# One stacked matmul of depth 96 instead of three for the destination term of a graph-network message

## The reference

```
m_in  = concat([x[src], x[dst], edge_attr])        # 200000 x 384
m     = silu(m_in @ msg_W1 + b1) @ msg_W2 + b2
agg   = segment_sum(m, dst)                        # sorted dst
x_new = LN(x + LN(x + mlp([x, agg])))
```

## Time and profile before

| | |
|---|---|
| median of three runs | 2572.13 us |
| span of the profiled execution | 2569.7 us |
| TensorE matmuls busy | 2182.9 us (85%), 21030 |
| weight loads busy | 1871.4 us (73%) |
| VectorE busy | 1577.3 us (61%) |
| ScalarE busy | 847.9 us (33%) |
| GpSimd busy | 1664.2 us (65%) |
| mean granted TensorE clock | 0.919 |
| DMA | 471.71 MB, mean 184 GB/s |

### The profile page before, as it was taken

How to read it: one execution, slowest core, us unless ns; L and a number is a source line. 1 busy time by engine, 2 the same in 40 slices (tenths; PEclk the granted TensorE clock), 3 DMA queues, 4 the chain that set the end, 5 groups by cost and what they waited for, 6 DMA issues and landing times. The chain is left out here.

```text
span 2569.7 us, 58924 instructions
## 1 busy us (share of the span) xinstructions
PE 2182.9 (85%) x21030; PEld 1871.4 (73%) x21030; DVE 1577.3 (61%) x4059; ACT 847.9 (33%) x1368; POOL 1664.2 (65%) x1618
## 2 busy tenths in 40 slices
PE   7898888888888988898889888988898878799996
PEld 7786777677777776776777776767677754699994
DVE  4786676667666766676667666766676647600005
ACT  3343333333333433333333333333333326200004
POOL 4777777777777777777777777777777755200002
PEclk9899999899899989998899999999999988899998
DMA  6555545554555555545554555455545543688871
GB/s 236 197 190 190 167 159 185 181 169 154 177 190 173 158 180 181 187 141 180 184 190 139 186 175 190 144 182 176 191 150 176 176 118 96 245 309 302 303 268 51
DMA packets 135225, 471.71 MB, mean 184 GB/s; under 512 B 55730, under 2 KB 77490, under 8 KB 113555
## 3 DMA queue, kind: packets, MB, share of 16 engines
q1 hardware_dynamic: 84586, 368.35, 41.1%
q0 software_dynamic: 50176, 102.86, 14.3%
q10 hardware_dynamic: 426, 0.03, 0.0%
HBM read 369.41 MB, written 101.70 MB: 183 GB/s over the span
## 5 line engine op out<-in xcount | busy, mean ns | idle before, releaser
L519 POOL DMA_INDIRECT gath<-P_d,src_i x1540 | 1543.2, 1002 | 469.4 <-issue 465.5
L650 PE MATMUL ps_pre<-wc,eT 128*128 128x128 f32 x3136 | 702.4, 306 | 13.7 <-DVE counts L567 13.7
L682 PE MATMUL ps_sum<-h,edgeN 128*128 128x129 f32 x3136 | 486.2, 302 | 265.7 <-ACT h L744 265.2
L590 DVE TENSOR_TENSOR pre<-ps_pre,gath 128x512 f32<-128x512 f32 x392 | 265.9, 678 | 588.6 <-issue 548.7
L682 PEld LDWEIGHTS ps_sum<-h,edgeN 128*128 128x128 f32 x3136 | 422.2, 209 | 278.1 <-ACT h L744 277.7
L744 ACT ACTIVATE h<-pre 128x512 f32<-128x512 f32 x392 | 247.9, 632 | 1122.2 <-DVE pre L590 1068.3
L666 PE MATMUL ps_cnt<-edgeK,edgeL 128*128 128x500 bf16 (+1 forms) x3136 | 585.1, 336 | 29.6 <-DVE edgeK L580 29.4
L580 DVE TENSOR_SCALAR edgeK<-iota,key 128x600 bf16<-128x600 f16 (+2 forms) x1568 | 526.4, 396 | 0.0
L652 PE MATMUL ps_pre<-Qw,nodeE 128*128 128x128 bf16 x4704 | 520.4, 220 | 0.0
L650 PEld LDWEIGHTS ps_pre<-wc,eT 128*128 128x128 f32 x3136 | 478.1, 192 | 32.6 <-issue 29.6
L666 PEld LDWEIGHTS ps_cnt<-edgeK,edgeL 128*128 128x128 bf16 x3136 | 320.1, 105 | 199.3 <-DVE edgeK L580 42.8
(11 more groups left out here) (128 smaller groups left out, 1021.4 us busy)
## 6 DMA issues: line engine op xcount, KB each, us to landing
eT<-eT SPq DMA_DIRECT2D x56, 1792.0 KB, 9.2
A_d<-counts SPq DMA_DIRECT2D x56, 1568.0 KB
A_c<-A_d SPq DMA_DIRECT2D x56, 1568.0 KB, 8.1
rel_b<-rel_d SPq DMA_DIRECT2D x56, 896.0 KB
gath<-P_d,src_i POOLq DMA_INDIRECT x1568
Qw<-Q_d SPq DMA_DIRECT2D x56, 96.0 KB
Q_d<-Qst SPq DMA_DIRECT2D x7, 672.0 KB, 7.8
xT_sb<-xT SPq DMA_DIRECT2D x7, 448.0 KB, 8.1
```

The lines of the kernel that those rows point to most:

```text
L519: pool.indirect_dma_start(gath[:, q, t * D:(t + 1) * D], None, v["P_d"], bass.IndirectOffsetOnAxis(ap=src_i[k][:, c:c + 1], axis=0)).then_ ...
L590: V.tensor_tensor(pre[x][:], ps_pre[x][:], gath[:, q, :], ALU.add).then_inc(pre_add, 1)
L650: T.matmul(o, eT[k][:, e0:e0 + P], wc[:], start=True, stop=False)
L682: last = T.matmul(ps_sum[k][:, 0:SW], edgeN[x][:, t, :], h[x][:, t, 0:SW], start=(q == 0 and t == 0), stop=(q == GQ - 1 and t == QT - 1))
```

## The change

Q_d keeps its layout. Instead of 128 table rows for a group, the kernel now loads 32 rows for each quad, at the quad's own first destination (qbase, a new row of 392 numbers), and puts the three bf16 parts below each other: part t on partitions 32t to 32t+31, so Qw is 96 x 7 x 128. rel_d counts from the quad's first destination, and nodeE has 96 partitions: partition p is compared with p mod 32 (pid is made by an integer iota and an AND), so each edge has three ones in its column. One matmul over 96 partitions then adds all three parts. The window is loaded by 7 register loads and 21 DMAs of 32 x 128 bf16.

The making of rel_d is cut for this into 98 rows of four quads. The core of the diff:

```
-        pid = sb("pid", [P, 1])
+        pid_i, pid = sb("pid_i", [P, 1], I32), sb("pid", [P, 1])
...
-            rel_b = sb("rel_b", [P, GE], BF16, both)
+            rel_b = sb("rel_b", [KQ, GE], BF16, both)
...
-    RP = 2 * GROUPS
-    RC = EP // RP
+    RP, RQ = 98, 4
+    RC = RQ * QT * P
...
-            V.tensor_scalar(relR[:], R_i[:, 0:RC], RB_i[:, 0:1], None, ALU.subtract).then_inc(rel_ready, 1)
+            V.tensor_tensor(rows4(relR[:]), rows4(R_i[:, 0:RC]),
+                            RB_i[:].unsqueeze(2).broadcast_to([RP, RQ, QT * P]), ALU.subtract).then_inc(rel_ready, 1)
...
+            V.tensor_scalar(qbase[:].rearrange("p (g q) -> p g q", q=GQ), F1, 0.0, float(NP_ - 1), ALU.max, ALU.min)
...
+        link(V.tensor_scalar(pid_i[:], pid_i[:], QW - 1, None, ALU.bitwise_and))
+        V.tensor_copy(pid[:], pid_i[:])
...
-    nodeE = [sb(f"nodeE{k}", [P, GE], BF16) for k in range(2)]
-    Qw = [sb(f"Qw{k}", [P, 3 * D], BF16) for k in range(2)]
+    nodeE = [sb(f"nodeE{k}", [KQ, GE], BF16) for k in range(2)]
+    Qw = [sb(f"Qw{k}", [KQ, GQ, D], BF16) for k in range(2)]
...
-            base = sp.value_load(gbase[0:1, bass.ds(g, 1)], min_val=0, max_val=NP_ - 1)
-            sp.dma_start(Qw[k][:], v["Q_d"][bass.ds(base, P), :]).then_inc(q_in[k], 16)
+            for q in range(GQ):
+                base = sp.value_load(qbase[0:1, bass.ds(g * GQ + q, 1)], min_val=0, max_val=NP_ - 1)
+                rows = v["Q_d"][bass.ds(base, QW), :].rearrange("r (t n) -> t r n", t=3)
+                for t in range(3):
+                    sp.dma_start(Qw[k][t * QW:(t + 1) * QW, q, :], rows[t]).then_inc(q_in[k], 16)
...
-                pe.wait_ge(q_in[k], 16 * (half + 1))
+                pe.wait_ge(q_in[k], 3 * GQ * 16 * (half + 1))
...
-                for part in range(3):
-                    last = T.matmul(o, nodeE[k][:, e0:e0 + P], Qw[k][:, part * D:(part + 1) * D],
-                                    start=False, stop=(part == 2))
+                last = T.matmul(o, nodeE[k][:, e0:e0 + P], Qw[k][:, q, :], start=False, stop=True)
```

More of the change, by code:

```diff
@@ L43 @@
 GW = 120
+QW = 32
+KQ = 3 * QW
 LASTQ = P - W0
@@ L82, in bass_gnn_two_layers @@
         gbase = sb("gbase", [1, GROUPS], I32)
+        qbase = sb("qbase", [1, QUADS], I32)
         ident = sb("ident", [P, P])
         identb = sb("identb", [P, P], BF16)
-        pid = sb("pid", [P, 1])
+        pid_i, pid = sb("pid_i", [P, 1], I32), sb("pid", [P, 1])
         iota = sb("iota", [P, 1000], F16)
@@ L146, in build_prepare @@
     P_d, Q_d, rel_d = v["P_d"], v["Q_d"], v["rel_d"]
-    pid, ident, identb, iota = v["pid"], v["ident"], v["identb"], v["iota"]
-    flag, offs, gbase = v["flag"], v["offs"], v["gbase"]
+    pid_i, pid, ident, identb, iota = v["pid_i"], v["pid"], v["ident"], v["identb"], v["iota"]
+    flag, offs, gbase, qbase = v["flag"], v["offs"], v["gbase"], v["qbase"]
     wab = sb("wab", [P, 2, D])
@@ L152, in build_prepare @@
     b1bc = sb("b1bc", [P, D])
-    RP = 2 * GROUPS
-    RC = EP // RP
-    R_i, RB_i, relR = sb("R_i", [RP, RC + 1], I32), sb("RB_i", [RP, 1], I32), sb("relR", [RP, RC], BF16)
+    RP, RQ = 98, 4
+    RC = RQ * QT * P
+    R_i, RB_i, relR = sb("R_i", [RP, RC + 1], I32), sb("RB_i", [RP, RQ], I32), sb("relR", [RP, RC], BF16)
     falls = sb("falls", [RP, RC], BF16)
@@ L189, in sync @@
         rows = v["dst_row"]
-        for h in range(2):
-            half = bass.AP(rows.tensor, rows.offset + h * RC, [[2 * RC, GROUPS], [1, RC + 1]])
-            sp.dma_start(R_i[h * GROUPS:(h + 1) * GROUPS, :], half).then_inc(r_in, 16)
+        sp.dma_start(R_i[:], bass.AP(rows.tensor, rows.offset, [[RC, RP], [1, RC + 1]])).then_inc(r_in, 16)
         for to, a in ((mw2, v["mW2"]), (v["u1a"], v["uW1"][0:D, :]), (u1b, v["uW1"][D:2 * D, :]), (v["u2"], v["uW2"])):
@@ L206, in sync @@
         sp.wait_ge(rel_ready, 1)
-        sp.dma_start(rel_d.rearrange("(g h c) -> h g c", h=2, c=RC)[0], relR[0:GROUPS, :]).then_inc(st_r, 16)
-        sp.dma_start(rel_d.rearrange("(g h c) -> h g c", h=2, c=RC)[1], relR[GROUPS:RP, :]).then_inc(st_r, 16)
+        sp.dma_start(rel_d.rearrange("(r c) -> r c", c=RC), relR[:]).then_inc(st_r, 16)
         for c in range(CHUNKS):
@@ L213, in sync @@
             if c == 1:
-                sp.wait_ge(st_r, 32)
-                sp.dma_start(v["rel_b"][:], rel_d[0:GE].partition_broadcast(P)).then_inc(v["r_in"], 16)
+                sp.wait_ge(st_r, 16)
+                sp.dma_start(v["rel_b"][:], rel_d[0:GE].partition_broadcast(KQ)).then_inc(v["r_in"], 16)
             if c == 3:
@@ L221, in gpsimd @@
     def gpsimd(pool):
-        pool.iota(pid[:], [[0, 1]], base=0, channel_multiplier=1, allow_small_or_imprecise_dtypes=True).then_inc(made, 1)
+        pool.iota(pid_i[:], [[0, 1]], base=0, channel_multiplier=1).then_inc(made, 1)
         pool.iota(iota[:], [[1, 1000]], base=0, channel_multiplier=0, allow_small_or_imprecise_dtypes=True).then_inc(made, 1)
@@ L279, in scalar @@
         firsts, lasts = v["dst_first"], v["dst_last"]
[L280 to L283, removed]
+        with nc.allow_non_contiguous_dma(reason="one word for each quad"):
+            act.dma_start(RB_i[:], firsts[0:TILES].rearrange("(r q t) -> r q t", q=RQ, t=QT)[:, :, 0]).then_inc(r_in, 16)
         act.dma_start(F_i[:], bass.AP(firsts.tensor, firsts.offset, [[GT, GROUPS], [1, GT + 1]])).then_inc(t_in, 16)
@@ L334, in checks @@
             V.memset(bad[:], 0.0)
[L335 to L336 removed]
+            dve.wait_ge(r_in, 32)
+            rows4 = lambda t: t.rearrange("p (q e) -> p q e", q=RQ)
+            V.tensor_tensor(rows4(relR[:]), rows4(R_i[:, 0:RC]),
+                            RB_i[:].unsqueeze(2).broadcast_to([RP, RQ, QT * P]), ALU.subtract).then_inc(rel_ready, 1)
             link(V.tensor_tensor(falls[:], R_i[:, 0:RC], R_i[:, 1:RC + 1], ALU.is_gt))
@@ L368, in checks @@
             V.tensor_scalar(gbase[:], F1[:, :, 0], 0.0, float(NP_ - 1), ALU.max, ALU.min)
+            V.tensor_scalar(qbase[:].rearrange("p (g q) -> p g q", q=GQ), F1, 0.0, float(NP_ - 1), ALU.max, ALU.min)
+        dve.wait_ge(made, 1)
+        link(V.tensor_scalar(pid_i[:], pid_i[:], QW - 1, None, ALU.bitwise_and))
+        V.tensor_copy(pid[:], pid_i[:])
         dve.wait_ge(b_in, 16)
@@ L400, in settled @@
         eng.wait_ge(st_z, 16)
-        eng.wait_ge(st_r, 32)
+        eng.wait_ge(st_r, 16)
         for stored, ring in ((st_p, PR), (st_q, QR)):
@@ L409, in build_edges @@
 def build_edges(nc, ctx, sem, sb, v):
-    flag, offs, gbase, force_general = v["flag"], v["offs"], v["gbase"], v["force_general"]
+    flag, offs, gbase, qbase, force_general = v["flag"], v["offs"], v["gbase"], v["qbase"], v["force_general"]
     pid, ident, identb, iota, wc = v["pid"], v["ident"], v["identb"], v["iota"], v["wc"]
@@ L478, in load_rel @@
         def load_rel(g):
-            sp.dma_start(rel_b[:], v["rel_d"][bass.ds(g * GE, GE)].partition_broadcast(P)).then_inc(r_in, 16)
+            sp.dma_start(rel_b[:], v["rel_d"][bass.ds(g * GE, GE)].partition_broadcast(KQ)).then_inc(r_in, 16)
         def store(g, k):
@@ L552, in expand @@
         def expand(k, cols):
-            return V.tensor_scalar(nodeE[k][:, cols], rel_b[:, cols], pid[:, 0:1], None, ALU.is_equal)
+            return V.tensor_scalar(nodeE[k][:, cols], rel_b[:, cols], pid[0:KQ, 0:1], None, ALU.is_equal)
         def expand_first(half, k, early=False):
```

## The result

| | before | changed |
|---|---|---|
| median us (lowest to highest, runs) | 2572.76 (2570.74 to 2574.09, 4) | 2751.97 (2748.25 to 2755.56, 4) |
| ratio, 95% interval | | 1.0694, 1.0678 to 1.071 |
| profiled run: time, span us | 2572, 2569.7 | 2750.08, 2748.2 |
| mean granted TensorE clock | 0.919 | 0.859 |
| last edge sums end, us | 2102.35 | 2282.47 |

The kernel is 6.9% slower; 2767 was forecast. The whole loss lies ahead of the last edge sums.

The account below looks back on a forecast made before the run. GpSimd's gathers bound the kernel at 36.6 us a group; the change makes a 39.8 us loop through SyncE's store, paid 54 times. With the later start, 195 us added to 2572.1 gives 2767 us, range 2690 to 2850.

Parts of the forecast that it names:

- SyncE's list: SyncE's issues after each group: 7 register loads and 21 DMAs add 14.5 us, so the store goes out at S+17.7.
- Rivals 3 and 4: Window loads: 0.71 us issue each, 2972 us (9%); or each waiting for the one before to land, near 4650 (2%).
- rival 4: Window loads: each small load waits for the one before to land, loop 75 us, time near 4650 us; chance 2%.
- The store's landing: Store of counts in each group: lands 13.0 us after its issue, and the next memset of counts waits for it.
- The loop: Each edge group: list, store, memset, rest of group (9.0 us) close a loop of 39.8 us, 3.2 above GpSimd's 36.6.
- One sign: Edge loop: GpSimd would now wait for adds, as one mark of the closed loop; no size given.
- The start: Prelude: longer lists start TensorE 13.9 us later, at 90.4; GpSimd loses 10.7 us; first S comes at 121.9.
- The sum: End of the last edge sums: 2296.9 us, 194.6 later than before, giving 2767 us in all.
- The matmuls: TensorE in the edge part: removed matmuls save 0.45 us a quad, 3.2 us a group, lying in spare time.
- rival 2: Edge part: TensorE's chain sets the pace, so the removed matmuls pay 176 us and the time is 2407; chance 5%.
- gathers' 36.6: GpSimd in the edge loop: a group's 28 gathers cost 36.6 us, the shortest group once its head start is used.
- rival 1: Edge loop: GpSimd stays the bound and only the start is paid, 2583 us, 0.4% slower; chance 14%.

Follow-up runs that it names:

- e1: Changed kernel with the store of counts issued right behind src_i, ahead of the window's 21 loads and eT: 2654.82 us, ratio 1.0326.
- e3: Kernel before the change, with 22 further register loads of SyncE ahead of the window's one load in each list: 2644.23 us, ratio 1.0284.
- e4: Kernel before the change, with only the first of the three bf16 matmuls of each tile, all loads kept: 2574.1 us, ratio 0.9998.
- e6: Changed kernel with seven 96-row loads a list, eT and the store ahead of them, and src_i and rel_b of group 1 earlier: 2647.94 us, ratio 1.0302.
- e12: e6 with VectorE building edgeK ahead of edgeN and edgeL for each quad, same DMAs: 2731.41 us, ratio 1.0633.
- e7: Kernel before the change, plus 21 loads of 32 x 128 into spare tiles behind the store in each list: 2570.5 us, ratio 0.9994.

## Why the prediction was right, step by step

**SyncE's list: right.** Forecast: store at S+17.7, measured S+17.15. The 21 loads with their register loads took about half a microsecond less than 14.5 more. Rivals 3 and 4 (0.71 us a load, serial landings) are out: the loads were issued 0.50 us apart, about as fast as the one large one. The section by which the prediction reads rival 4 (the Trainium skill, "DMA: Bandwidth & Descriptors", Anatomy of one DMA) is headed as the path of DMAs that GpSimd issues; these are SyncE's, so rival 4 is out by the trace alone.

**The store's landing: right,** 12.87 for 13.0. It shares the DMA engines with eT (300 GB/s, above), as before.

**The loop: right.** 9.03 for 9.0 from memset to next S, TensorE restarting at 2.09 us for its sums as in the earlier trace rows; 53 pitches from 129.78 to 2214.99 are 39.34 each, for 39.8. That the store's wait is a cause, and not only a companion, e1 (wait away: -97 us) and e3 (delay alone, in the kernel before: a wait of 262 us and +72 us of time) show from both sides. One sign did not come as forecast: GpSimd waits for adds only 39 us in all (4.0 before), most of it early.

**The start: half right.** TensorE began at 88.5 (forecast 90.4), the first gather behind the first add at 92.86 (93.1). The first S came at 129.78, not 121.9. A term was missing: rel_b of group 1 stands behind both windows' loads on SyncE, and group 0's second half is queued behind it on VectorE:

```profile
105.33 17.16 SPq L486 DMA_DIRECT2D rel_b<-rel_d  x2
```

```profile
116.85 0.68 DVE L560 TENSOR_SCALAR nodeE<-rel_b,pid 96x1792 bf16<-96x1792 bf16 x1 [10.90 <-DMA rel_b<-rel_d]
```

**The sum.** 2296.9 was forecast for the end of the last sums. Start +7.9, loops 53 x (39.34 - 39.8) = -24, the last two groups 67.5 us for 65.6, +2: 2282.3, for 2282.5 measured. The two errors have opposite signs, so a part of the closeness, some 10 of 24 us, is luck.

**The matmuls: right,** and rival 2 is out: e4 takes two thirds of these products away and gains nothing.

**Where the reasoning fell short: "gathers' 36.6".** I took GpSimd's pitch for a constant and the loop for the one limit, and rival 1 (2583) rested on it. In the changed kernel 28 gathers of 1.109 + 0.30 us take 39.5 us, no less than the loop. GpSimd's head start (from a group's first gather to its first add) is 29 us at group 10 and about 15 us from group 26 on; in the kernel before it is 7 us from group 6 on, all used up. So in the changed kernel the loop alone sets the pitch, and the adds wait only 8.0 us for gathers. But the second limit lies right under it, which the prediction did not see, and that it did not come out above the loop is luck too. Whoever mends only the loop finds it: e1 and e6 end at 2655 and 2648, not near 2583.

**Why gathers lengthen.** VectorE and GpSimd around one such gather of the changed kernel:

```profile
1109.51 0.67 DVE L584 TENSOR_TENSOR edgeN<-iota,rel_g 128x512 f32<-128x512 f16 x1
1109.73 3.10 POOL L526 DMA_INDIRECT gath<-P_d,src_i  x1 [0.30 <-issue]
1110.11 0.67 DVE L585 TENSOR_TENSOR edgeL<-iota,low 128x512 bf16<-128x512 f16 x1
1110.71 1.30 DVE L587 TENSOR_SCALAR edgeK<-iota,key 128x1000 bf16<-128x1000 f16 x4
1112.61 0.69 DVE L597 TENSOR_TENSOR pre<-ps_pre,gath 128x512 f32<-128x512 f32 x1 [0.60 <-PE ps_pre L658]
```

In the trace of before, gathers that start 0.1, 0.3 and 0.5 us behind the start of edgeN take 1.40, 1.20 and 1.00 us: they all end 1.5 us behind it. Those that start at 0.7, 0.9 and 1.1 take 1.40, 1.19 and 1.03 and all end at 2.1. Those at 1.2 and 1.3 take the undisturbed 0.94 again. Two lines of one of the first kind:

```profile
692.42 0.68 DVE L577 TENSOR_TENSOR edgeN<-iota,rel_g 128x512 f32<-128x512 f16 x1
692.73 1.19 POOL L519 DMA_INDIRECT gath<-P_d,src_i  x1 [0.30 <-issue]
```

So a gather that begins beside edgeN or edgeL does not run slower, it ends at a moment that VectorE sets, and the traces give that moment. The gather just shown ends 0.82 us behind the end of edgeN. In the kernel before, all 212 edge-part gathers (from group 1 on) of over 1.06 us end 0.82 us (within 0.01) behind the end of a VectorE instruction, nearly always of edgeN or edgeL; in the changed kernel 304 of 342 do. Its gather of 3.10 us above ends 0.82 us behind the end of the last edgeK (1110.71 + 1.30), and the one shown of e12 as long behind the end of edgeL. It looks as if a gather is held at its start until VectorE lets it go, and then does the rest of its 0.94 us. In 28 further ones of the changed kernel, and in 37 of e6's 57 long ones, the end stands 0.95 us behind one edgeK and 0.12 behind the last; why was not sorted out. In the changed kernel, gathers that begin beside edgeN or edgeL hold 243 of the 254 us that gathers lose there, and those that begin while VectorE is idle take 0.944 us on average. With edgeK first (e12), 36 of the 37 long ones begin beside edgeK, with edgeN and edgeL right behind it.

The Trainium skill, "SBUF — State Buffer", Who interferes with whom, says that VectorE and GpSimd share one pair of ports under an exclusive lock, that a two-input VectorE operation from SBUF (against a GpSimd instruction that reads SBUF) or one in a two-port mode takes part of it, and that the one which comes first holds it for its whole instruction, the other being blocked and not throttled; the ends at fixed moments agree with that. The same section reports that tensor_tensor did not stall DMAs that GpSimd issues; here it goes with longer ones, 1.19 us beside edgeN in the lines above, and the measurement decides.

e12 shows that VectorE's order alone moves the gathers' mean by 43 ns. It does not show which port is held. Why the changed kernel meets the bad moments ten times as often as before (100 long ones for 9) is not shown. That it depends on how VectorE's sequence falls against the gathers' beat of 1.25 us is argued from e12. In the kernel before, fewer products (e4) or more loads (e7) alone do not change the mean, and a late list (e3) does; which part of the change keeps it at 1045 ns in e6, the fewer products or the window's loads, was not found.

## What to carry to other kernels

Price a change by what its instructions do to the queue that issues them, before what they save: here 392 x 0.45 us of TensorE work lay in idle time, while 14 us of SyncE's issue time stood ahead of a store that the next group waits for. Put a transfer on which a buffer's reuse depends at the head of its queue; here that alone gave back 97 of 179 us. And take the second limit's duration as a variable: an operation on GpSimd may be longer in the changed kernel although it is the same instruction.

## What was not expected of the hardware

- One gather took 944 ns undisturbed and up to 3.21 us in the changed kernel and 3.90 us in e6; the mean over a kernel lay between 1000 and 1109 ns, and 83 us of time hung on the order of three VectorE operations.
- The lengthened gathers of the kernel before, all 212, end 0.82 us behind the end of a VectorE instruction.
- Seven loads of 96 rows cost SyncE 13.22 us, 21 of 32 rows 14.19: joining loads did not save issue time.
- Loads of 8 KB each, 21 in a group, put behind the store (e7), left the time of the kernel before where it was (0.9994).
- On one chip the kernel before took 3080 us, on three others 2571 to 2573.
